# State layer of a vision tower in 32 steps of one batch and channel block, with narrow products in column groups

## What is computed

```python
h = h + _L0_ffn_ref(_layernorm(h), ...)          # the FP4 layer
h = h + _L1_attn_ref(_layernorm(h), ...)         # the state layer

def _L1_attn_ref(x, w_in, b_in, w_conv, b_conv, w_xproj, w_dt, b_dt, w_out):
    xz = x @ w_in.T + b_in                       # 256 -> 512 (xc) and 512 (z)
    xc, z = jnp.split(xz, 2, axis=-1)
    xc = conv1d(xc, w_conv, 4 taps, causal, one filter a channel) + b_conv
    xc = jax.nn.silu(xc)
    x_dbl = xc @ w_xproj.T                       # 512 -> 32
    delta = jax.nn.softplus(xc @ w_dt.T + b_dt)  # 512 -> 16
    A = jnp.exp(-jnp.abs(x_dbl[..., :16]) * delta)
    Bx = x_dbl[..., 16:] * delta * xc[..., :16]
    # h_t = A_t * h_(t-1) + Bx_t over the tokens; then y = h * z[..., :16]; y @ w_out.T
```

## Time and profile before

| | us |
|---|---|
| median of three runs (lowest, highest) | 2016.27 (2015.23, 2020.01) |
| the profiled execution | 2018.79 |
| its span, first to last instruction | 2017.1 |

### The profile page before, as it was taken

One profiled execution on the slowest core, in us unless ns is written; L12 is line 12 of the kernel. 1 busy time (PEld: TensorE's weight loads), 2 busy tenths in 40 slices (PEclk: granted clock), 3 DMA queues, 4 the chain that ended last, 5 costly groups with the idle time before them and its releaser, 6 DMA issues. The chain is left out here.

```text
span 2017.1 us, 36263 instructions
## 1 busy us (share of the span) xinstructions
PE 1833.6 (91%) x10746; PEld 1204.9 (60%) x10746; DVE 1480.3 (73%) x4020; ACT 939.5 (47%) x2132; POOL 965.1 (48%) x1658
## 2 busy tenths in 40 slices
PE   6997997999899999799999699599799699999997
PEld 5886774444688888577777333388677233333332
DVE  3334896777477777699998498577798589998981
ACT  1112564666121121344443244355444477777777
POOL 3554564666333333233333111088743776666663
PEclk9997998999799999899999799699899699999999
DMA  4330668887100000695000200067786344443320
GB/s 134 117 117 27 163 167 207 162 173 144 48 1 1 1 1 1 270 413 232 1 1 1 65 10 10 29 157 200 193 254 204 69 107 101 102 106 92 88 68 28
DMA packets 241706, 215.01 MB, mean 107 GB/s; under 512 B 117210, under 2 KB 216188, under 8 KB 241404
## 3 DMA queue, kind: packets, MB, share of 16 engines
q1 hardware_dynamic: 227804, 183.51, 34.1%
q0 software_dynamic: 9408, 25.70, 3.9%
q10 hardware_dynamic: 4320, 3.70, 0.7%
HBM read 108.04 MB, written 103.12 MB: 105 GB/s over the span
## 5 line engine op out<-in xcount | busy, mean ns | idle before, releaser
L2918 ACT ACTIVATE attend_w<-ps 128x512 f32<-128x512 f32 x512 | 279.9, 598 | 91.2 <-PE ps L2785 67.1
L3121 DVE TENSOR_REDUCE attend_mx<-ps 128x1 f32<-128x512 f32 x448 | 281.7, 682 | 36.1 <-PE ps L2773 26.5
L2785 PE MATMUL ps<-keep_o,keep_x 99*128 99x512 bf16 x512 | 191.9, 384 | 2.4 <-ACT attend_w L2918 2.4
L2773 PE MATMUL ps<-keep_x,keep_o 96*128 96x512 bf16 x448 | 173.3, 387 | 8.0 <-DVE attend_mx L3121 6.3
L987 POOL TENSOR_TENSOR keep_early<-keep_early,first_causal 128x128 f32<-128x128 f32 x256 | 110.9, 456 | 77.7 <-ACT keep_early L961 76.7
L1009 DVE SCALAR_TENSOR_TENSOR keep_early<-ps,first_causal 128x512 f32<-128x512 f32 (+3 forms) x256 | 111.4, 486 | 44.8 <-PE ps L901 44.0
L2803 PE MATMUL ps<-attend_w,keep_early 128*17 128x512 f32 x1024 | 136.0, 600 | 0.0
L1215 PE MATMUL ps<-mlp_zT,keep_early 128*128 128x128 f32 x1056 | 128.2, 280 | 8.0 <-ACT mlp_zT L1257 8.0
L961 ACT ACTIVATE keep_early<-ps 128x512 f32<-128x512 f32 (+3 forms) x256 | 97.0, 435 | 74.6 <-PE ps L901 74.0
L1215 PEld LDWEIGHTS ps<-mlp_zT,keep_early 128*128 128x128 f32 x1056 | 121.9, 194 | 16.0 <-ACT mlp_zT L1257 16.0
L2773 PEld LDWEIGHTS ps<-keep_x,keep_o 96*128 96x128 bf16 x448 | 43.8, 98 | 144.9 <-DVE attend_mx L3121 105.1
(11 more groups left out here) (405 smaller groups left out, 4483.1 us busy)
## 6 DMA issues: line engine op xcount, KB each, us to landing
sorted<-keep_x SPq DMA_DIRECT2D x3, 14720.0 KB, 75.2
tok_xin<-in_xk SPq DMA_DIRECT2D x64, 256.0 KB, 2.6
qk_parts<-qkv_parts SPq DMA_DIRECT2D x33, 384.0 KB, 3.2
qk_parts<-moe_parts SPq DMA_DIRECT2D x32, 384.0 KB
sorted<-moe_zn POOLq DMA_DIRECT2D x64, 128.0 KB, 3.2
moe_zs<-sorted SPq DMA_DIRECT2D x45, 128.0 KB, 3.2
keep_o<-qk_parts SPq DMA_DIRECT2D x14, 384.0 KB, 4.4
keep_x<-qk_parts SPq DMA_DIRECT2D x14, 384.0 KB, 5.6
```

Source lines behind the costliest of these rows:

```text
L2773: nc.tensor.matmul(ps[:, bank, :], qs[0:R, x.buf(0), h, t * P:(t + 1) * P], ks[0:R, x.buf(0), h, :], start=True, stop=True).then_inc(s_msc, 1)
L2785: nc.tensor.matmul(ps[:, SC + i % RING, :], ks[:, x.buf(2), HG * g + j, kt * P:(kt + 1) * P], qs[:, x.buf(2), HG * g + j, :], start=True, ...
L2918: nc.scalar.activation(w[:, j, kt % 2, :], ps[:, SC + (HG * k + j) % RING, :], ACT.Exp)\
L3121: nc.vector.tensor_reduce(mx[:, t, k:k + 1], ps[:, MX + (at + 1) % RING, :], AX, ALU.max)\
```

## The change

The work of `pass_ssm_in` is cut into 32 steps `g`, one batch and one channel block each. In step `g` TensorE projects block `g`, turns tile `g + 6` and multiplies the states of block `g - 2`; ScalarE applies silu to block `g - 2`, copies tile `g + 5`, normalizes tile `g + 7` and takes block `g` out of PSUM twice: once with its bias into `xb`, once times the last tap into `cv`. VectorE adds the other three taps and takes statistics of tile `g + 8`. The products with few output columns (z, now 32 columns `ZW` wide, and the states, padded from 48 to 64 columns `PW`) are laid into groups of columns of the array, side by side, each with its own part of the tokens: four groups of 128 tokens for z (`ZT`), two of 256 for the states (`PT`). SP therefore moves z in four DMAs a batch and the states in six; x stays one. The loops over batches are written out.

The first five tiles (`FIRST`) are normalized in `pass_fp4`, in its tiles 12 to 23, into a part of `env.o`: `bn_stats` on VectorE, four POOL operations for all five, five activations on ScalarE. The class tokens get buffers of their own (`zT0`, `xs0`, `z0`, `pr0`), and their DMAs are waited for by SP alone. At the end ScalarE runs one `Exp` on a single column (`warm`) ahead of the last states' copy.

```diff
@@ pass_fp4, ScalarE, in the loop over tiles, after take_hT
+                if 0 <= s - FIRST_AT - FIRST - 2 < FIRST:
+                    i = s - FIRST_AT - FIRST - 2
+                    if i == 0:
+                        act.wait_ge(s_frs, 1)
+                    nc.scalar.activation(first[:, i, :], env.h[:, i, :], ACT.Identity, bias=f_nb[:, i:i + 1],
+                                         scale=f_rs[:, i:i + 1])
@@ pass_fp4, VectorE, in the loop over tiles, after add_h
+                if 0 <= s - FIRST_AT < FIRST:
+                    dve.wait_ge(s_h, s - FIRST_AT + 1)
+                    nc.vector.bn_stats(f_st[:, s - FIRST_AT, :], env.h[:, s - FIRST_AT, :]).then_inc(s_fbn, 1)
+                if s == FIRST_AT + FIRST:
+                    dve.wait_ge(s_fbn, FIRST)
+                    nc.vector.memset(env.gap[0:1, :], 0.0)
+                    for i in range(FIRST):
+                        last = nc.vector.bn_aggr(f_mv[:, i, :], f_st[:, i, :])
+                    last.then_inc(s_fstat, 1)
@@
+FIRST, FIRST_AT = 1 + TB, 12
+ZW, PW = 2 * DS, 4 * DS
@@ pass_ssm_in
+    ZT, PT = P // ZW, P // PW
+    GT = MI * B
+    LAG = 2
...
@@ SyncE
+            def batch(b):
+                rows = slice(b * DS, (b + 1) * DS)
+                sp.wait_ge(s_z16, b + 2)
+                for j in range(ZT):
+                    sp.dma_start(env.planes[rows, Z_IN, 1 + P * j:1 + P * (j + 1)], z16[ZW * j:ZW * j + DS, :]).then_inc(s_oz, 16)
+                sp.wait_ge(s_xs, MI * (b + 1) + 1)
+                sp.dma_start(env.planes[rows, X_IN, 1:SEQ], xs[0:DS, 0, :]).then_inc(s_ox, 16)
+                sp.wait_ge(s_prs, b + 2)
+                n = S // PT
+                for j in range(PT):
                     for c in range(3):
+                        sp.dma_start(env.planes[rows, c, 1 + n * j:1 + n * (j + 1)],
+                                     pr[PW * j + DS * c:PW * j + DS * (c + 1), :]).then_inc(s_op, 16)
...
@@ TensorE
+            def gate(b):
+                pe.wait_ge(s_z16, b + 1)
+                for k in range(KD):
+                    for j in range(ZT):
+                        last = nc.tensor.matmul(ps[ZW * j:ZW * (j + 1), Z16, 0:P], w_in[:, k, DI:DI + ZW],
+                                                zT[:, b % 2, k, P * j:P * (j + 1)], start=(k == 0), stop=(k == KD - 1),
+                                                skip_group_check=True, tile_position=(0, ZW * j))
+                last.then_inc(s_zin, 1)
+            def states(g):
+                b, m = g // MI, g % MI
+                if m == 0:
+                    pe.wait_ge(s_prs, b + 1)
+                pe.wait_ge(s_xs, MI + g + 1)
+                n = S // PT
+                for j in range(PT):
+                    last = nc.tensor.matmul(ps[PW * j:PW * (j + 1), PR, 0:n], w_pr[:, m, :], xs[:, m, n * j:n * (j + 1)],
+                                            start=(m == 0), stop=(m == MI - 1), skip_group_check=True, tile_position=(0, PW * j))
+                last.then_inc(s_st, 1)
...
+            for g in range(GT):
+                if g == 1:
+                    first_states()
+                project(g)
+                if g == 0:
+                    turn(FIRST)
+                if g + 6 < NT:
+                    turn(g + 6)
+                if g % MI == 1:
+                    gate(g // MI)
+                if g >= LAG:
+                    states(g - LAG)
...
@@ ScalarE
+            def take_in(g):
+                m = g % MI
+                act.wait_ge(s_in, MI + g + 1)
+                past(act, s_cv, g - MI + 1)
+                nc.scalar.activation(xb[:, m, H:H + S], ps[:, X0 + m, :], ACT.Identity, bias=col(env, "b_in", m)).then_inc(s_xb, 1)
+                past(act, s_xs, MI + g - MI + 1 if g >= MI else 0)
+                nc.scalar.activation(cv[:, m, :], ps[:, X0 + m, :], ACT.Identity, bias=b_tap[:, m:m + 1], scale=last_tap(m))\
+                    .then_inc(s_tap, 1)
+            def silu(g):
+                b, m = g // MI, g % MI
+                act.wait_ge(s_cv, g + 1)
+                past(act, s_st, MI + g - MI + 1 if g >= MI else 0)
+                if m == 0:
+                    past(act, s_ox, 16 * b)
+                nc.scalar.activation(xs[:, m, :], cv[:, m, :], ACT.Silu, bias=col(env, "b_conv", m)).then_inc(s_xs, 1)
...
+            for g in range(GT + LAG):
+                if g >= LAG:
+                    silu(g - LAG)
+                if g >= LAG + MI and (g - LAG) % MI == 0:
+                    take_states((g - LAG) // MI - 1)
+                if g < GT:
+                    if FIRST <= g + 5 < NT:
+                        take_zT(g + 5)
+                    if FIRST + 2 <= g + 7 < NT:
+                        apply(g + 7)
+                    take_in(g)
...
+            nc.scalar.activation(warm[:, :], env.eps[:, :], ACT.Exp)
+            take_states(B - 1)
@@ VectorE
+            def convolve(g):
+                m = g % MI
+                ch = Chain(dve, c_dve, (DC - 2) * g)
+                dve.wait_ge(s_tap, g + 1)
+                if g < MI:
+                    dve.wait_ge(s_xb, MI + g + 1)
+                for j in range(DC - 1):
+                    ins = nc.vector.scalar_tensor_tensor(cv[:, m, :], xb[:, m, j:j + S], col(env, "w_conv", DC * m + j), cv[:, m, :],
+                                                         ALU.mult, ALU.add)
...
+            for s in range(FIRST, FIRST + 3):
+                stats(s)
+            for g in range(GT):
+                convolve(g)
+                if g + FIRST + 3 < NT:
+                    stats(g + FIRST + 3)
```

More of the change, by code:

```diff
@@ L1658, in _ @@
+            first_token()
+            batch(0)
+            sp.wait_ge(s_o0, 80)
             sp.dma_start(env.planes[:, :, 0:1], io["ssm"].rearrange("c r t -> r c t"), allow_slow_non_contiguous=True).then_inc(s_o0, 16)
-            for b in range(B):
+            for b in range(1, B):
                 batch(b)
[L1661 to L1664, removed]
+            sp.wait_ge(s_o0, 96)
@@ L1682, in project, with turn @@
[L1682 to L1687, removed]
[L1688 to L1694 removed]
+            def turn(s):
+                if s >= FIRST:
+                    pe.wait_ge(s_z, s - FIRST + 1)
+                past(pe, s_zT, s - 1)
+                src = first[:, s, :] if s < FIRST else z[:, s % 3, :]
+                for k in range(KD):
+                    last = nc.tensor.transpose(ps[:, T0 + s % 2, k * P:(k + 1) * P], src[:, k * P:(k + 1) * P], env.ident[:, :])
+                last.then_inc(s_T, 1)
@@ new lines, in first_project, with first_gate @@
+            def first_project(m):
+                if m == 0:
+                    pe.wait_ge(s_zT, 1)
+                for k in range(KD):
+                    last = nc.tensor.matmul(ps[:, X0 + m, 0:B], w_in[:, k, m * P:(m + 1) * P], zT0[:, k, :],
+                                            start=(k == 0), stop=(k == KD - 1))
+                last.then_inc(s_in, 1)
+            def first_gate():
+                for k in range(KD):
+                    last = nc.tensor.matmul(ps[0:ZW, Z16, 0:B], w_in[:, k, DI:DI + ZW], zT0[:, k, :],
@@ new lines, in _ @@
+            turn(0)
+            turn(1)
+            for m in range(MI):
+                first_project(m)
+                if m + 2 < FIRST:
+                    turn(m + 2)
+            first_gate()
+            for g in range(GT):
[10 more added lines that the diff above has]
+                    states(g - LAG)
@@ L1719, in _ @@
+            for g in range(GT - LAG, GT):
+                states(g)
         @block.scalar
@@ new lines, in take_states @@
+            def take_states(b):
+                act.wait_ge(s_st, MI * (b + 2))
+                past(act, s_op, 48 * PT * b)
+                nc.scalar.copy(pr[:, :], ps[:, PR, 0:S // PT]).then_inc(s_prs, 1)
+            take_zT(0)
+            take_zT(1)
+            take_zT(2)
+            for m in range(MI):
+                first_in(m)
+                if m + 3 < FIRST:
+                    take_zT(m + 3)
+            act.wait_ge(s_zin, 1)
+            nc.scalar.activation(z0[:, :], ps[0:ZW, Z16, 0:B], ACT.Identity, bias=b_z[0:ZW, :]).then_inc(s_z16, 1)
@@ new lines, in _ @@
+            apply(FIRST)
+            apply(FIRST + 1)
+            for g in range(GT + LAG):
[9 more added lines that the diff above has]
+                    take_in(g)
+                if g == 1:
+                    act.wait_ge(s_st, MI)
+                    nc.scalar.copy(pr0[:, :], ps[0:PW, PR, 0:B]).then_inc(s_prs, 1)
+                if g % MI == 2 and g < GT:
+                    take_gate(g // MI)
```

289 lines of the change are left out of this document (122 added, 167 removed).

## The result

The changed kernel takes 2051.14 us (median of three executions; 2050.09 to 2055.70) against 2016.59 us of the kernel before on the same chip: a ratio of 1.0175 with an interval of 1.015 to 1.0199. The forecast was 1973 us, a gain of 43 us; what came is a loss of 35, under 2% and clear of the spread. The profiled execution of after is the one of 2051.14 us, with a span of 2049.2 us.

The account below looks back on a forecast made before the run. VectorE bounded the state layer's batch (14.3 of 15.8 us busy). Stage end 42.7 us earlier, table load -1.2, FP4 layer +0.5: -43.4 us, from a median of 2016.3 to 1973 us, range 1964 to 1988.

Parts of the forecast that it names:

- 3.0 us for a full step: State layer's full pipeline: three engines at 2.83 to 2.95 us a step, hand-offs hidden by lags; 24 such steps, 72.0 us.
- SP's and silu's: State layer: silu waits for the previous batch's x DMA in SP's queue; 9.0 us against 12.0 a batch, costs nothing.
- The engines' sums: State layer, work per step: VectorE 2.83 us, ScalarE 2.8 to 2.95, TensorE 2.93.
- The column groups: TensorE's narrow products run side by side: states 0.63 us a step, gate 0.63 us a batch.
- rival B: Narrow products run one after another: TensorE 3.5 us a step, 1985 to 1987 us; chance 0.08.
- The start: State layer's beginning: first full projection at 1129, first convolution at 1135, pipeline full at 1140 us.
- The end: State layer after the last input at 1224.8: taps, silu, states, last copy at 1229.8, six DMAs; stage ends at 1235.2.
- Around it: Neighbouring stages: early table load gives back 1.2 us, FP4 layer's extra work costs 0.5 us.
- the table load: ScalarE's next table, loaded early at the state layer's end, gives the next stage 1.2 us; other bound 0.
- the FP4 layer's additions: Five tiles' statistics and normalizations moved into the FP4 layer cost 0.5 us; bounds 0 and 4.1.
- Rival D: TensorE stays at its lower clock through the stage: some 5.4 us a step, 34 us slower, 2050 us; chance 0.04.
- Rival A: ScalarE becomes the bound at 3.45 us a step: 12.3 us more, 1985 us; chance 0.22.

Follow-up runs that it names:

- ahead5: The changed kernel with VectorE's statistics five tiles ahead instead of three, their buffers five deep: 1969.06 us, ratio 0.9761 to the kernel before.
- ahead5_plain: The changed kernel with statistics five tiles ahead and the narrow products without column groups, five SP DMAs a batch: 1989.35 us, ratio 0.9862 to the kernel before.
- ahead5_pow: The changed kernel with statistics five tiles ahead and GpSimd's power operation done twice: 1970.47 us, ratio 0.9771 to the kernel before.
- ahead4: The changed kernel with statistics four tiles ahead instead of three, four buffers: 1985.98 us, ratio 0.9842 to the kernel before.

## Why the prediction was wrong, step by step

- **The step that failed** is this sentence: "With lags of two steps between them a hand-off costs latency and not rate, as long as none is late", with the "3.0 us for a full step" that I took from it. I looked at how many steps ahead each engine's data is made, and not at what stands in front of it in each queue. `stats(g + 8)` is four steps or more ahead of the projection that needs the tile, but `apply(g + 8)` is put one step later in front of `take_in(g + 1)`, so for the reads the lead is zero. The sum had 24 full steps at 3.0, 72 us; the runs showed 25 steps at 6.11, 152.6 us, on a wait that the sum put at nothing. Its terms were at hand: taps and statistics in the earlier trace rows, normalization and reads in the earlier trace rows; GpSimd's chain, the one term between them, I priced nowhere. I did walk one such loop, SP's and silu's, and found it harmless (it was: ScalarE waits for no DMA in the state layer of after or ahead5); this one I didn't walk.
- **The engines' sums held.** VectorE 2.83 us a step, ScalarE 2.8 to 2.95, TensorE 2.93 were forecast; where these decide (ahead5) the step is 2.80 on the mean, so TensorE's sum was a little high. ahead5 takes 1969 us, where 1973 was forecast for the step as I meant it; its stage is 6 us shorter than the sum, about half of it from the start and half from the steps.
- **The column groups held.** The states' four records take 0.65 us (forecast 0.63) and the gate's sixteen 0.64 (0.63): groups run beside each other, rival B is out. The page "TensorE: Matmul & The Clock Gate", Part 3, of the Trainium skill lets a weight load overlap with running products only where it aims at other rows. Here the trace differs: it has four loads for the same rows within 0.20 us, beside the products. The page "TensorEngine Tiling (Array Packing)", Key Properties, of the Trainium skill has the change of mode drain the engine. The trace allows for that: two passes of 0.21 in 0.65 leave the 0.2 us of the prediction and no more. Rival B's price was near: without groups ahead5_plain takes 1989, where 1985 to 1987 was worked out.
- **The start** was 3 us better than forecast (1125.99 to 1129). A good third of that is that a turn and a narrow projection together take 1.17 us (turns at 1122.08, 1123.25, 1124.43), where I had summed 0.66 and 0.90 one behind the other; the rest is a beginning 0.6 us earlier (1120.81), the first two turns (0.63 us for both) and the gate.
- **The end** held: from the last copy's end to the next stage it is 5.4 us, as forecast; SP's six issues take 3.67 us, 0.61 each, where 0.59 was forecast.
- **Around it:** the table load saves 1.1 us in the one pair of traces (forecast 1.2); the FP4 layer's additions cost nothing that shows: its last addition ends at 1120.2 us before, at 1119.7 in after and between 1118.3 and 1121.7 in the other traces, so a cost of the 0.5 forecast can't be told.
- **Rival D** gave 2050 us and "slower", with an end of the stage at 1312 (measured 1311.75), and its point of decision, 4.3 us a step, is right arithmetic: at 6.1 the change loses. That its numbers came out is luck, since its mechanism isn't what happened. The clock in after was 0.72 to 0.92 in the stretches of the ring, where TensorE waits in every step, and the step was 6.1 in each; with the ring broken the clock is 1.00. Rival A's price is out: in ahead5 ScalarE is busy 59.1 of 60 us, and a step is 2.80 us, not 3.45.
- **The chances.** 0.95 for faster rested on three engine sums. None of the rivals was a wait that closes a loop over three engines, and so "slower" had only D's 0.04.

## What to carry to other kernels

Before a pipeline's step is forecast from its busiest engine, walk every loop of waits through the queues in issue order: what stands in front of the awaited instruction on its engine, back to the start, and divide the sum by the steps over which the loop closes. A step made "n ahead" of its reader has a lead of zero for anything issued behind it in the same queue. Where such a loop closes within one step, break it first: here a longer lead gave 82 us and two lines in another order 59, and only then did the work saved on the engines show.

## What the runs showed of the hardware that was not expected

GpSimd's small operations take longer when they begin while one of VectorE's taps runs. The power operation on 128x1, group by line: first after (stretch 1145 to 1200 us, VectorE idle when it runs), then ahead5 (VectorE's taps beside it).

```profile
L1898 POOL TENSOR_TENSOR ssm_rs<-ssm_ve,keep_mhalf 128x1 f32<-128x1 f32 x9 | 5.0, 550 | 0.7
```

```profile
L1898 POOL TENSOR_TENSOR ssm_rs<-ssm_ve,keep_mhalf 128x1 f32<-128x1 f32 x20 | 18.9, 946 | 1.6
```

The same instruction takes 550 and 946 ns; the first addition goes from 191 to 558, while the taps on VectorE stay at 0.75 us. Within one kernel (ahead5_plain) the power operation takes 0.92 us beside taps (1161.52) and 0.55 without (1164.66). The beginning decides, not the overlap: in the traces of the changed kernel and its eight variants, each of the 128 power operations that begin while a tap runs ends 0.41 us after the end of that tap, and each of the other 180 takes 0.55, even where a tap begins right behind it and runs beside most of it (1164.11 in ahead5_pow). ScalarE's work makes no difference: in ahead4 the operation at 1161.29 takes 0.55 with ScalarE busy all the while. Why, no run here shows.
